# V of the small heads from the whole array: rows kept twice, and new orders on VectorE and ScalarE

## The reference

```python
x = x + _L0_attn_ref(_layernorm(x), ...)                 # self attention, scores * exp(-|decay| * distance)
x = x + _L0_xattn_ref(_layernorm(x), ctx, ctx, mask...)  # cross attention, 4 key/value heads, causal + mask
# in both, per sequence:
q, k, v = rows @ Wq.T + bq, rows @ Wk.T + bk, rows @ Wv.T + bv
scores = einsum('bhsd,bhtd->bhst', q, k) / sqrt(8)       # 16 heads, 64 x 64
out = einsum('bhst,bhtd->bhsd', softmax(scores), v)
```

## Time and profile before

| | |
|---|---|
| time, median of 3 runs | 1889.69 us (1885.44 to 1890.2) |
| profiled execution: span | 1940.8 us |
| PE, PEld busy over the span | 1657.9 us (85%), 1377.0 us (71%) |
| DVE, POOL, ACT busy over the span | 1471.5 us (76%), 1406.9 us (72%), 961.1 us (50%) |
| small-head attentions, first to last work | about 23.6 to 612 us of the span |
| granted TensorE clock, mean | 0.929 |

### The profile page before, as it was taken

How to read it: one execution, slowest core, us unless ns; L and a number is a source line. 1 busy time by engine, 2 the same in 40 slices (tenths; PEclk the granted TensorE clock), 3 DMA queues, 4 the chain that set the end, 5 groups by cost and what they waited for, 6 DMA issues and landing times. The chain is left out here.

```text
span 1940.8 us, 63428 instructions
## 1 busy us (share of the span) xinstructions
PE 1657.9 (85%) x24717; PEld 1377.0 (71%) x24719; DVE 1471.5 (76%) x3151; ACT 961.1 (50%) x2012; POOL 1406.9 (72%) x1253
## 2 busy tenths in 40 slices
PE   4999999999998826699999999999998689267776
PEld 2777777777776725577777888888887579267675
DVE  6888888888886771688998888888887566845454
ACT  3677777777774322354445444444444441234343
POOL 3777777877785455688989988888887358656655
PEclk9999999999997957799999999999999789678888
DMA  8000032000000042444443443343343156521211
GB/s 248 10 7 8 8 120 73 18 17 15 15 16 3 1 136 70 104 120 114 120 120 96 97 97 97 97 97 96 96 98 83 52 180 197 161 69 58 61 55 41
DMA packets 155071, 154.03 MB, mean 79 GB/s; under 512 B 37246, under 2 KB 106944, under 8 KB 154160
## 3 DMA queue, kind: packets, MB, share of 16 engines
q1 hardware_dynamic: 140528, 130.91, 24.9%
q0 software_dynamic: 6704, 15.61, 2.8%
q10 hardware_dynamic: 7696, 5.71, 1.1%
HBM read 58.77 MB, written 26.71 MB: 44 GB/s over the span
## 5 line engine op out<-in xcount | busy, mean ns | idle before, releaser
L1437 POOL TENSOR_TENSOR wa_rot<-wa_rot,wa_cross 128x1024 f32<-128x1024 f32 x128 | 305.3, 2385 | 51.1 <-DVE wa_cross L1649 50.8
L412 POOL TENSOR_TENSOR sa_sd<-sa_sd,sa_mx 128x1024 f32<-128x1024 f32 x128 | 243.5, 1903 | 133.1 <-DVE sa_mx L648 132.2
L592 ACT ACTIVATE sa_sd<-sa_sd 128x1024 f32<-128x1024 f32 x128 | 135.7, 1060 | 114.5 <-POOL sa_sd L412 111.5
L1646 DVE TENSOR_TENSOR wa_rot<-wa_ps_qk,cos 128x1024 f32<-128x1024 f32 x128 | 155.7, 1217 | 40.2 <-PE wa_ps_qk L1503 40.1
L1602 ACT COPY wa_pt<-wa_ps_svt 128x1024 f32<-128x1024 f32 x64 | 64.9, 1014 | 229.4 <-PE wa_ps_svt L1539 229.4
L648 DVE TENSOR_REDUCE sa_mx<-sa_sd 128x16 f32<-128x1024 f32 x128 | 156.2, 1220 | 4.4
L1443 POOL TENSOR_TENSOR wa_sd<-wa_sd,wa_mx 128x1024 f32<-128x1024 f32 x64 | 121.9, 1905 | 38.2 <-DVE wa_mx L1662 38.2
L534 PEld LDWEIGHTS sa_ps_o<-sa_vbd,sa_pt 128*64 128x64 f32 x4096 | 132.9, 140 | 19.7 <-issue 12.0
L534 PE MATMUL sa_ps_o<-sa_vbd,sa_pt 128*64 128x18 f32 x4096 | 145.7, 214 | 0.8 <-DVE sa_o L675 0.8
L1503 PE MATMUL wa_ps_qk<-wa_xt,l_wk 128*128 128x128 f32 x1024 | 133.5, 284 | 11.7 <-DVE wa_cross L1649 11.6
L419 POOL TENSOR_TENSOR sa_km<-sa_k,head_mask 128x512 f32<-128x512 f32 x128 | 135.4, 1058 | 7.3 <-ACT sa_k L583 6.9
(11 more groups left out here) (312 smaller groups left out, 4311.9 us busy)
## 6 DMA issues: line engine op xcount, KB each, us to landing
wa_whole<-wa_rot SPq DMA_DIRECT2D x1024, 64.0 KB, 2.0
choice_dram<-sa_zero_rows SPq DMA_DIRECT2D x32, 256.0 KB, 3.4
choice<-choice_dram SPq DMA_DIRECT2D x32, 256.0 KB, 3.6
x_res<-in_x_dram SPq DMA_DIRECT2D x16, 256.0 KB, 6.8
sa_ctx_t<-in_ctx_t_dram SPq DMA_DIRECT2D x64, 64.0 KB, 1.8
c_index<-in_index_dram SPq DMA_DIRECT2D x2, 2048.0 KB, 7.8
xn_dram<-c_xn SPq DMA_DIRECT2D x16, 256.0 KB, 2.9
cs_ctx_t<-in_ctx_t_dram SPq DMA_DIRECT2D x16, 256.0 KB, 3.0
```

The lines of the kernel that those rows point to most:

```text
L412: pool.tensor_tensor(sd[:, v % 4], sd[:, v % 4], mx[:, v % 4].unsqueeze(2).to_broadcast([P, H0, SEQ]), ALU.subtract).then_inc(sub_ready, 1)
L592: act.activation(sd[:, v % 4], sd[:, v % 4], ACT.Exp, scale=scale).then_inc(p_ready, 1)
L1437: pool.tensor_tensor(rot[n][:, v % 2], rot[n][:, v % 2], cross[n][:], ALU.add)\
L1646: dve.tensor_tensor(rot[n][:, v % 2].rearrange("p f j t -> p (f j) t"), src.rearrange("p f j t -> p (f j) t"), bc(k.cos[:], 1, 2 * QUADS), ...
```

## The change

Four things are edited.

1. V on the whole array. `xt` and `ctx_t` now hold each sequence's rows twice, side by side, and the 128 columns of weights that they make give V on all 128 partitions in one matmul per sequence. `wv` is the plain 128×128 matrix. For self attention `x_copy` writes the doubled `xt` (256 elements per partition, where it wrote 128). For cross attention the doubled rows come from a new input in DRAM, and each load is 128 KB instead of 64 KB.
2. The V copy is two instructions on 64 partitions and 128 elements each, one for each parity of heads, where it was one on 128 partitions and 256 elements.
3. New orders inside a step on ACT and DVE.
4. `zero_rows`, the source of the zero stores, is half as large (ZEROED is 2), so there are 64 stores of 128 KB instead of 32 of 256 KB. And one wait more for PE, at a single item.

```diff
-        xt = sb("xt", [P, 2, P])
+        xt = sb("xt", [P, 2, 2, 2, SEQ])
-        ctx_t = sb("ctx_t", [P, 4, P])
+        ctx_t = sb("ctx_t", [P, 4, 2, 2, SEQ])
-        ZEROED = 4
+        ZEROED = 2
...
-                sp.dma_start(ctx_t[:, t % 4, :], k.in_ctx_t[t]).then_inc(ctx_loaded[t % 4], 16)
+                sp.dma_start(ctx_t[:, t % 4], k.in_ctx_twice[t]).then_inc(ctx_loaded[t % 4], 16)
...
+                if isinstance(n, int) and n == NT + 7:
+                    pe.wait_ge(x_added, NT)
...
-                pe.matmul(ps_kv[:, 0], wk[:], kv, start=True, stop=True)
+                pe.matmul(ps_kv[:, 0], wk[:], kv[:, :, 0], start=True, stop=True)
                 for b in range(2):
-
-                    for half in range(2):
-                        mm = pe.matmul(ps_kv[half * SEQ:(half + 1) * SEQ, 1 + b], kv[:, b * SEQ:(b + 1) * SEQ],
-                                       wv[:, half], start=True, stop=True)
+                    mm = pe.matmul(ps_kv[:, 1 + b], kv[:, b].rearrange("p h s -> p (h s)"), wv[:], start=True, stop=True)
...
-                act.copy(xt[:, v % 2], xt_ps).then_inc(xt_ready, 1)
+                act.copy(xt[:, v % 2], bc(xt_ps.rearrange("p (b s) -> p b s", b=2), 2, 2)).then_inc(xt_ready, 1)
...
-                act.copy(vbd[:, v, :, :, :, 0:D0], ps_kv[:, 1:3].rearrange("p b (n h d) -> p b n h d", h=2, d=D0))\
-                   .then_inc(v_ready, 1)
+                v_ps = ps_kv[:, 1:3].rearrange("p b (n h d) -> p b n h d", h=2, d=D0)
+                for half in range(2):
+                    rows = slice(half * SEQ, (half + 1) * SEQ)
+                    op = act.copy(vbd[rows, v, :, :, half, 0:D0], v_ps[rows, :, :, half])
+                op.then_inc(v_ready, 1)
...
-                for stage, behind in ((exponential, 5), (o_copy, 8), (x_copy, 1), (kv_copy, 2), (p_copy, 6),
-                                      (normalise, 0)):
+                for stage, behind in ((o_copy, 8), (x_copy, 1), (p_copy, 6), (kv_copy, 2), (normalise, 0),
+                                      (exponential, 5)):
...
-                for stage, behind in ((aggregate, 9), (softmax, 4), (residual, 8), (sums, 8), (q_copy, 2), (divide, 7)):
+                for stage, behind in ((weigh, 4), (q_copy, 2), (maximum, 4), (residual, 8), (aggregate, 9), (sums, 8),
+                                      (invert, 7), (divide, 7)):
```

More of the change, by code:

```diff
@@ L485, in project @@
                     pe.wait_ge(centred, 3)
-                pe.matmul(ps_q[:, 0:P], wq[:], xt[:, v % 2], start=True, stop=True).then_inc(q_made, 1)
+                pe.matmul(ps_q[:, 0:P], wq[:], xt[:, v % 2, :, 0], start=True, stop=True).then_inc(q_made, 1)
                 if late(n, 1):
@@ L628, in _, with weigh @@
         def _(dve):
-            def softmax(n, t, v, cross):
+            def weigh(n, t, v, cross):
                 dve.wait_ge(s_made, n + 1)
@@ L646, in softmax, with maximum @@
                     dve.tensor_tensor(by_group[:, 2:4], s_ps[:, 2:4], decays, ALU.mult).then_inc(s_taken, 1)
+            def maximum(n, t, v, cross):
                 dve.wait_ge(s_taken, n + 1)
@@ L663, in keep_folds, with invert, divide @@
                 dve.tensor_tensor(k.f0_rw_centred[:], k.f0_rw[:], score_ps, ALU.subtract).then_inc(centred, 1)
-            def divide(n, t, v, cross):
+            def invert(n, t, v, cross):
                 dve.wait_ge(o_made, n + 1)
                 dve.reciprocal(rec[:, v % 2], o_ps[:, :, D0]).then_inc(rec_ready, 1)
+            def divide(n, t, v, cross):
                 if late(n, 2):
@@ L2380, in build @@
         k.in_x, k.in_mask, k.in_ctx_t, k.in_dist, k.in_dd = a["x"], a["mask"], a["ctx_t"], a["dist"], a["dd"]
+        k.in_ctx_twice = a["ctx_t_twice"]
         k.in_ctx, k.xx_dram = a["ctx"], a["xx_dram"]
@@ L2470, in build @@
                 k.head_mask = r0("head_mask", [P, GRP, 1], src=a["head_mask"])
-                k.a_wq, k.a_wk, k.a_wo, k.x_wq, k.x_wk, k.x_wo = (
-                    r0(n, [P, P], src=a[n]) for n in ("a_wq", "a_wk", "a_wo", "x_wq", "x_wk", "x_wo"))
-                k.a_wv, k.x_wv = (r0(n, [P, 2, P], src=a[n]) for n in ("a_wv", "x_wv"))
+                k.a_wq, k.a_wk, k.a_wv, k.a_wo, k.x_wq, k.x_wk, k.x_wv, k.x_wo = (
+                    r0(n, [P, P], src=a[n]) for n in ("a_wq", "a_wk", "a_wv", "a_wo", "x_wq", "x_wk", "x_wv", "x_wo"))
                 k.a_bq, k.a_bk, k.a_bv, k.x_bq, k.x_bk, k.x_ln_g, k.x_ln_b = (
@@ L2548, in _layout @@
     o["ctx_t"] = v["ctx_1024"].reshape(NT, P, P).transpose(0, 2, 1)
+    o["ctx_t_twice"] = np.repeat(o["ctx_t"].reshape(NT, P, 2, 1, SEQ), 2, axis=3)
     W, b = v["L0_attn_Wqkv_w"], v["L0_attn_Wqkv_b"]
@@ L2563, in _layout @@
     o["x_wo"], o["x_bo"] = v["L0_xattn_Wo"].T, v["L0_xattn_bo"].reshape(1, P)
[L2564 to L2569, removed]
     o["x_ln_g"], o["x_ln_b"] = v["L0_xattn_ln_g"].reshape(P, 1), v["L0_xattn_ln_b"].reshape(P, 1)
```

## The result

The changed kernel takes 1876.81 us (median of 4 runs, 1875.89 to 1880.23), the kernel before 1889.95 (4 runs, 1885.44 to 1894.39): ratio 0.9928, interval 0.9904 to 0.9952. That is 13 us less, where 18 were forecast. The forecast of 1872 has the right sign and its range holds the time, but one of its two large terms came out at nothing.

A forecast was written before the change was run, and what follows sets the result against it. Self attention was bound by PE's list tied with the PE-ACT-PE chain, cross attention by the chain alone. Gains of 10.8, 5.4 and 1.5 made 17.7 us: 1889.7 to 1872 us, 8-in-10 range 1859 to 1886.

The forecast's parts named there:

- V on PE: V's matmuls on PE: two changes of weight form go, saving 0.25 and 0.05, so x_transpose comes 0.30 us earlier.
- The rival by which V gains nothing on PE: Changes of form on PE would move, not go; only cross attention and the first steps gain: 1883 us, chance 0.05.
- p_copy ahead of kv_copy: ACT's order: p_copy ends at 3.96 us in the self-attention step, so scores could start at 4.21, below 4.39.
- the chain: PE to ACT to PE, from scores through x_transpose and p_copy to the next scores; 4.57 us in self attention before.
- DVE's order: q copy moved into DVE's hole before the maximum: no cost or gain in steady steps, some 1.5 us gained early.
- x_copy holds out_project: Self attention: doubled x_copy ends 0.12 us later and delays out_project, so the step is 4.39, 0.18 saved.
- the ring: p_transpose, p_copy, k, V copies, normalise, exponential, next step's p_transpose: 4.25 us, hidden in self attention, binding cross attention at 4.26.
- The exponential at the end of the step: Exponential last on ACT: the next step's p_transpose waits for it; cross attention falls only from 4.35 to 4.26 us.
- The neutral rival: Half a V copy on ACT costs as much as the whole, 0.26 us; 4.47 binds both halves: 1887 us, chance 0.12.
- Self attention: Self-attention steps from 60 us on: 57 items save 0.19 us each, together 10.8 us.
- First items: First ten items, with extra statistics work on DVE: filled holes give 0.15 us each, 1.5 us (bounds 0 and 3).
- Stores and loads: 64 half-size zero stores take 22 to 44 us; the context load behind them costs 0, at worst 3 us once.

The follow-up runs named there:

- V alone: Kernel before with V on the whole array, doubled x_copy, V copied in halves and 128 KB stores, but old orders on ACT and DVE: ratio 1.0048.
- the kernel with normalise ahead: Changed kernel with normalise moved ahead of p_copy in ACT's order, no longer between the V copies and the exponential: ratio 0.9845 to the kernel before.
- the second profile: The changed kernel, unedited, run and profiled again on another chip (B), against the kernel before on that chip: ratio 0.9914.

## Why the prediction was right, and where not

- **V on PE** (0.30 earlier for x_transpose): right in its mechanism and nearly in size, 0.28. Two changes of form went, and the passes stayed at 0.11. The Trainium skill's rule of the drain ("TensorEngine Tiling (Array Packing)", Key Properties) agrees with this trace: 0.16 behind a change, 0.11 without. The rival by which V gains nothing on PE fell; but V alone made the kernel 9.6 us slower, since ACT's copies cost more than PE gained.
- **p_copy ahead of kv_copy**: right, the chain no longer binds. With the new V and the exponential first it gave 0.18 in self attention and 0.27 in cross attention, together with DVE's order, which by itself carried nothing in the changed kernel.
- **x_copy holds out_project** (4.39 in self attention): the hold is real, 0.15 from x_copy's end to out_project in the kernel with normalise ahead, but in the changed kernel it is hidden. That the mean came out as the forecast said is luck in part: two of four steps are the ring's 4.36, and the other two, 4.85 and 3.98, the mask's, which the forecast did not price. Without the ring the steps away from the mask are 4.26 to 4.33, because values to scores needs 1.04, not 1.16; the 1.16 of the earlier trace rows contained p_copy's chain.
- **The exponential at the end of the step**: the ring was named, and it binds in cross attention and in half of the self steps. Its size was the failed step: "I take 0.15, the row of the same count, so 0.30 for both" measured 0.57, and "0.25 back to PE" measured 0.05. The 0.30 is right for 128 partitions (0.31 measured); what it had wrong is that 64 partitions cost as little. The neutral rival had the price of a half nearly right (0.265 from one half to the next, 0.57 for both). Its ring of 4.47 did not come because of the second error, which pulled the other way: 4.25 + 0.27 − 0.20 = 4.32, and the other 0.04 is p_transpose with its way to ACT (1.13 for 1.10) and roundings. So cross attention's 60 × 0.09 = 5.4 us came out at 0, which is the 5 us between forecast and result.
- **Self attention**: 57 × 0.19 = 10.8 forecast, 57 × (4.60 − 4.41) = 10.8 measured. First items: the traces are 3.3 us apart at the start of the 14th maximum (96.3 and 93.0), 0.8 of it already at the first; forecast 1.5. With the second profile's 94.5 the 3.3 are 1.8, so the size is not shown.
- **DVE's order**: cost nothing and gained nothing in the steady steps, as forecast. The 1.5 us of the first items, which the forecast gave to its filled holes, are not its: with the old order the 14th maximum starts just as early.
- **Stores and loads**: no PE wait for a context load. But the cover nearly went. SP's waits of the changed kernel, 250 to 340 us, and its zero stores (ns min/median/max, first and last start):

```profile
SPq L395 <- PE sa_ps_kv L496: 33.1, 8, 5.0
```

```profile
L391 SPq DMA_DIRECT2D choice_dram<-sa_zero_rows x64: 323/451/1952, 263.6 to 301.0; - x64
```

The burst grew from 22 to 38 us, near the bound of the same time each, and the longest wait behind it, the cover, shrank from 21.6 to 5.0 us.

## What to carry to other kernels

When an instruction is moved to the end of an engine's step, look for the ring that it closes with the next step's first use of its result: add its full length to the starts between, on both engines, and compare it with the step. Such a ring has to be priced for each half of the work, since a gain in one can be eaten in the other, and an entry that has no business in it should be moved into the wait that the ring itself leaves on the engine (normalise: 13 us by moving one entry of a table). A split of an instruction by partitions must be priced as two whole ones until a row shows otherwise. When two kinds of step alternate, look at the single steps too: a mean can fit a forecast for a reason that the forecast does not contain.

## What the runs showed of the hardware

- A COPY on ACT from PSUM with 128 elements takes 0.265 us to the next start on 64 partitions and about 0.15 on 128, with the same pattern, and gaps in its source make no difference. Two such copies took 0.57 on 64 partitions and 0.31 on 128, one of 256 elements on 128 partitions 0.26 (0.25 by the median). Why half the partitions cost more is open.
- Normalise, an ACT instruction of 128 columns with a scale and a bias per partition, took 0.40 us to the next start; cut into two of 64 columns it took 0.68, 0.28 more.
- A DVE instruction with int32 in and bf16 out took 0.42 us where it started ahead of POOL's subtraction, which then took 2.01 instead of 1.90. Started during a POOL instruction it ended 0.28 us behind that instruction's end in 205 of 207 cases (0.32 in the other two), so that its median was 0.45 in the kernel before, 0.77 in the changed one and 1.80 in the one with the mask made earlier. It stood until POOL was done, and did not run slower beside it; POOL's own time was 1.90 in those cases. The Trainium skill, page "Perfetto Trace Analysis", section Optimizing Scalar/DVE Operations, says that the two engines share an SBUF read port; the traces agree with it, but no run here shows that it is the port.
- The way from a record's end on ACT to the waiting start on PE was 0.05 to 0.06 us for the exponential and p_transpose, and 0.25 for p_copy and scores. What makes the difference was not tried.
